# One matmul per distinct piece in the state picks, and the FFN tiles' transposes two blocks later

## What is computed

```python
def cell(h, x):
    gi = x @ W_ih + b_ih
    gh = h @ W_hh + b_hh
    i_r, i_z, i_n = jnp.split(gi, 3, axis=-1)
    h_r, h_z, h_n = jnp.split(gh, 3, axis=-1)
    r = jax.nn.sigmoid(i_r + h_r)
    z = jax.nn.sigmoid(i_z + h_z)
    n = jnp.tanh(i_n + r * h_n)
    h_new = (1.0 - z) * n + z * h
    return (h_new, h_new)
...
qx, sx, sc = _reorder_quantize_x(xf, up_reorder_index)
g = _qlinear(qx, sx, sc, w_gate, up_reorder_index, out_idx=down_reorder_index)
u = _qlinear(qx, sx, sc, w_up, up_reorder_index, out_idx=down_reorder_index)
t = jax.nn.silu(g) * u
qt, st, sct = _reorder_quantize_x(t, down_reorder_index)
y = _qlinear(qt, st, sct, w_down, down_reorder_index)
...
x = x + y
```

## Time and profile before

| what | us |
|---|---|
| median of 3 runs (2846.30 to 2849.53) | 2847.83 |
| the profiled execution | 2844.01 |
| its span, first to last instruction | 2842.2 |
| TensorE matmul busy in it | 2554.6 |
| VectorE busy | 1686.3 |
| GpSimd busy | 1252.9 |
| ScalarE busy | 1139.7 |
| one-add product of t = 2, 3, 4, 5 (from the first pick to the last block) | 98.4, 101.8, 99.5, 105.0 |

### The profile page before, as it was taken

The page is one execution under the profiler, slowest core; times in us unless marked ns, Lnnn a source line. Parts: engine busy times, 40 slices in busy tenths (PEclk is TensorE's granted clock), DMA queues, the critical chain, the costliest instruction groups (busy, mean ns, idle before and its releaser), DMA issues. The chain is left out here.

```text
span 2842.2 us, 154419 instructions
## 1 busy us (share of the span) xinstructions
PE 2554.6 (90%) x67605; PEld 1655.8 (58%) x67605; DVE 1686.3 (59%) x3398; ACT 1139.7 (40%) x2317; POOL 1252.9 (44%) x598
## 2 busy tenths in 40 slices
PE   2088999999989999999999999999896999999996
PEld 1066777777767778777665664755642444444442
DVE  8852222224822222225737879867492888888887
ACT  1312222225722222225602333323233777777774
POOL 0256666663146666665161450713601233333334
PEclk8599999999999999999999999999998999999998
DMA  6833222224622222225664353443432223232322
GB/s 196 241 82 82 71 72 74 71 71 107 146 69 71 72 74 71 71 75 138 191 143 122 109 144 113 125 153 97 146 121 95 71 86 95 79 96 84 95 64 54
DMA packets 234857, 293.97 MB, mean 103 GB/s; under 512 B 69581, under 2 KB 194023, under 8 KB 233895
## 3 DMA queue, kind: packets, MB, share of 16 engines
q1 hardware_dynamic: 212743, 240.84, 31.3%
q10 hardware_dynamic: 18304, 36.19, 3.7%
q0 software_dynamic: 3680, 15.21, 1.9%
HBM read 231.61 MB, written 60.45 MB: 103 GB/s over the span
## 5 line engine op out<-in xcount | busy, mean ns | idle before, releaser
L1161 PE MATMUL psum<-second_shared 64*32 64x384 f16 x32768 | 1029.5, 325 | 48.1 <-issue 28.3
L1169 PE MATMUL psum<-low_w,low_hot 64*32 64x384 f16 x16384 | 819.1, 325 | 5.6 <-issue 5.6
L1407 DVE TENSOR_SCALAR second_shared<-psum 32x384 f16<-32x384 f32 x496 | 272.4, 549 | 754.1 <-PE psum L1161 746.8
L1161 PEld LDWEIGHTS psum<-second_shared 64*32 64x32 f16 x32768 | 594.5, 93 | 209.6 <-issue 78.8
L971 POOL TENSOR_TENSOR low_hot<-first_shared,sum_mask 128x1024 f16<-128x1024 f16 x256 | 504.5, 1971 | 425.0 <-DVE first_shared L1394 165.4
L965 POOL TENSOR_TENSOR second_shared<-first_shared,whole_mask 128x2048 f16<-128x2048 f16 x128 | 462.3, 3612 | 447.3 <-PE psum L1161 352.3
L1061 ACT ACTIVATE second_shared<-psum 32x384 f16<-32x384 f32 x496 | 239.4, 483 | 807.5 <-PE psum L1161 801.5
L1249 PE MATMUL psum<-low_w,low_hot 64*64 64x384 f16 x12288 | 513.9, 325 | 12.6 <-issue 6.5
L1249 PEld LDWEIGHTS psum<-low_w,low_hot 64*64 64x64 f16 x12288 | 373.9, 108 | 146.2 <-issue 10.0
L1169 PEld LDWEIGHTS psum<-low_w,low_hot 64*32 64x32 f16 x16384 | 315.7, 93 | 66.3 <-issue 7.1
L2037 PE MATMUL psum<-first_shared,hT 128*64 128x256 f32 (+1 forms) x1856 | 314.6, 492 | 0.0
(11 more groups left out here) (286 smaller groups left out, 2667.5 us busy)
## 6 DMA issues: line engine op xcount, KB each, us to landing
low_w<-w_rows SPq DMA_DIRECT2D x384, 144.0 KB
low_w<-w_rows SPq DMA_DIRECT2D x256, 120.0 KB
second_shared<-w_rows SPq DMA_DIRECT2D x1024, 24.0 KB, 1.8
x_gates<-x_out ACTq DMA_DIRECT2D x58, 384.0 KB, 2.4
xg<-x_gates SPq DMA_DIRECT2D x58, 384.0 KB, 3.2
low_w<-w_rows SPq DMA_DIRECT2D x256, 72.0 KB
low_w<-w_rows SPq DMA_DIRECT2D x384, 48.0 KB
w_rows<-quantised SPq DMA_DIRECT2D x24, 384.0 KB, 4.9
```

The costliest lines, as they stand in the source:

```text
L1161: last = nc.tensor.matmul(run[m][u][j * Q:(j + 1) * Q, :], whole_hot[rows[u], m, sign, kk, j % 2 * Q:(j % 2 + 1) * Q], whole_w[rows[u], m, ...
L1169: nc.tensor.matmul(run[m][u][j * Q:(j + 1) * Q, :], low_hot[rows[u], m, kk, j % 2 * Q:(j % 2 + 1) * Q], low_w[rows[u], m, at:at + UC], sta ...
L1407: last = nc.vector.tensor_scalar(whole_w[u * B:u * B + Q, m, 0, bq, :], run[m][u][bq * Q:(bq + 1) * Q, :], 1.0 / HIGH_ONE, None, ALU.mult)
```

## The change

Two things. First, in the picks of t = 2 to 5 the kinds that occur several times, A0 (four rows) and A1H (three rows), get a selector of their own, sum_sel, which holds the ones of all their rows; A2H keeps its window into low_sel. A pick is then three matmuls instead of eight, with the same sum. sum_sel lies in the part of quantised (qdn) that holds the rounded w_down from t = 5 on. GpSimd fills it between the two pair products, with a memset and 14 casts, and the first pick waits for it (sel_ok). Second, turn_pair and turn_down are called inside a four, ahead of its third block, instead of ahead of the first.

```diff
+            SUM_KINDS = (A0, A1H)
+            sum_sel = qdn[:, 0:2 * PB * P // D, :].rearrange("p k n -> p (k n)").rearrange("p (a g r) -> p a g r", a=2, g=PB)
...
+                sel_ok = ssem("sel_ok")
...
                         pair_hots(0)
+                        pool.wait_ge(hot_ok, block_no(2, 0, 0) + 1)
+                        nc.gpsimd.memset(sum_sel, 0.0).then_inc(sel_ok, 1)
+                        pool.wait_ge(sel_ok, 1)
+                        eights = ident[:].rearrange("p (n k) -> p n k", k=SK)
+                        for r, kind in enumerate(SUM_ROWS):
+                            if kind in SUM_KINDS:
+                                for sub in range(SUBS):
+                                    at = sub * B + r * SK
+                                    nc.gpsimd.tensor_copy(sum_sel[:, SUM_KINDS.index(kind), :, at:at + SK], eights[:, sub::SUBS, :]).then_inc(sel_ok, 1)
                         pair_hots(1)
...
                         def sum_chain(t, m, behind=None):
-                            def four(n, ahead):
+                            def four(n, ahead, turn_tile=None):
 
                                 for j in range(BUFS):
+                                    if turn_tile and j == BUFS // 2:
+                                        turn_tile()
...
-                                turn_pair(first)
-                                four(2, 0)
+                                four(2, 0, lambda: turn_pair(first))
                                 with pe.Fori(first + 1, tiles[-1] + 1) as tile:
-                                    turn_pair(tile)
-                                    four(tile, 2 - first)
+                                    four(tile, 2 - first, lambda: turn_pair(tile))
                             else:
                                 with pe.Fori(0, KD) as n:
-                                    turn_down(n)
-                                    four(n, 2)
+                                    four(n, 2, lambda: turn_down(n))
                                 turn_columns()
...
                         def pick(t, first=0, last_one=None):
                             pe.wait_ge(cut_h, CUTS * t)
+                            if t == FINE:
+                                pe.wait_ge(sel_ok, 1 + SUBS * sum(kind in SUM_KINDS for kind in SUM_ROWS))
                             for n in range(first, places(t) if last_one is None else last_one):
                                 group, whole = pick_of(t, n)
                                 if whole:
-                                    shift, kinds, pick_rows = WHOLE_SEL, WHOLE_ROWS, whole_sel[:, group]
+                                    rows = [(kind, whole_sel[:, group, WHOLE_SEL - r * SK:WHOLE_SEL - r * SK + P]) for r, kind in enumerate(WHOLE_ROWS)]
+                                elif t < FINE:
+                                    rows = [(kind, low_sel[:, group, LOW_SEL - r * SK:LOW_SEL - r * SK + P]) for r, kind in enumerate(LOW_ROWS)]
                                 else:
-                                    shift, kinds, pick_rows = LOW_SEL, LOW_ROWS if t < FINE else SUM_ROWS, low_sel[:, group]
+                                    rows = [(kind, low_sel[:, group, LOW_SEL - r * SK:LOW_SEL - r * SK + P]) for r, kind in enumerate(SUM_ROWS)
+                                            if kind not in SUM_KINDS]
+                                    rows += [(kind, sum_sel[:, n_kind, group, :]) for n_kind, kind in enumerate(SUM_KINDS)]
...
-                                for row, kind in enumerate(kinds):
-                                    last = nc.tensor.matmul(psum[:, SEL_BANKS[n % SELS], 0:KD * B], pick_rows[:, shift - row * SK:shift - row * SK + P],
+                                for r, (kind, pick_rows) in enumerate(rows):
+                                    last = nc.tensor.matmul(psum[:, SEL_BANKS[n % SELS], 0:KD * B], pick_rows,
                                                             a_split[:, kind].rearrange("p g b -> p (g b)"),
-                                                            start=row == 0, stop=row == len(kinds) - 1)
+                                                            start=r == 0, stop=r == len(rows) - 1)
                                 last.then_inc(selected, 1)
```

## The result

The kernel with the change takes 2824.27 us in the median of five runs (2817.68 to 2830.37), the kernel before 2846.30 beside it. The ratio is 0.9928, 95% interval 0.9905 to 0.9950: 20.5 us faster, with 14 to 27 in the interval (the two medians alone are 22.0 apart). The forecast was 2828.6, 19.2 us faster. The total came out as forecast; three of its terms did not (less waiting for tiles than forecast, more slow clock, less gain at t = 2), and their errors nearly cancel.

What follows compares the result with a forecast made beforehand. TensorE was taken to set the end through the products of t = 2 to 5. Picks 12.2, transposes 7.0 and 0 for the rest make 19.2 us, so 2847.8 - 19.2 = 2828.6 us; range 2819 to 2840.

Steps and rivals of the forecast that it cites:

- Picks, behind blocks 0 and 1: Picks 3 to 7 of t = 2 to 5: 25 matmuls fewer save 2.9 us a product.
- Ahead of block 0: Picks 0 to 2: ScalarE's store holds the start at t = 3 to 5; only t = 2 gains 0.58 us.
- Transposes: Each tile's turn is asked for 5.26 us later: 7.0 us of TensorE's 14.1 us of tile waits go.
- 39.3 us: VectorE's time from the end of tile 1 to tile 4 at t = 3, leaving 1.2 us of waiting.
- At t = 5: Four w_down tiles: VectorE falls back 9.4 us with 4.7 in hand, leaving 4.7 us of waits instead of 7.3.
- Clock: Four start gaps and one tile wait make 2 falls to 1.2 GHz, 3.4 us, as many as now: net 0.
- two in five: Share of TensorE waits of 2.41 to 2.74 us followed by the lower clock; one fall costs 1.7 us.
- The start gap: TensorE's wait ahead of block 0 grows from 1.41 us to 2.5 to 2.8, in four places.
- The third rival: Every start gap ahead of block 0 drops the clock: 6.8 us instead of 2.7, time 2832.7; chance 0.10.
- Selectors: GpSimd's memset and 14 casts take 3 to 30 us, hidden in an idle stretch of 94.05 us: cost 0.
- The second rival: VectorE runs in the slow order, 13.98 us a tile, with 15.2 us of waits: 8.4 us gained, 2839.4; chance 0.15.
- the prediction's sign that t = 0 and 1 don't move: The prediction is wrong if the products of t = 0 and 1 move.

Runs made afterwards that it cites:

- the two kernels with less lead: The change with the transposes ahead of a four's second block, or in the middle of it: ratios to the kernel before 0.9947 and 0.9936.
- the two kernels above: The change with t = 5's w_down transposes two blocks later still, or ahead of blocks 10, 15, 21, 26: ratios to the kernel before 0.9928 and 0.9890.
- the kernel with w_down two blocks later: The change with the four w_down transposes of t = 5 two blocks later still: ratio to the kernel before 0.9928.

## Why the prediction was right, and where not

For t = 3 to 5 the prediction's terms make 8.7 + 7.0 + 0 = 15.7 us, and 15.8 were measured. As measured below, the terms are 8.9 + 9.5 - 3.4 = 15.0, with 0.8 us not placed; that the sums are so near is luck. By its steps:

**Picks, behind blocks 0 and 1.** 2.9 us a product forecast, 2.70 to 2.73 in each of the four. Right: the next hot was there, and no wait stands at block 1 or 3. Ahead of block 0, nothing was forecast at t = 3 to 5 and 0.24 us each was found; ScalarE's store holds the start nearly, not wholly. The wait for it inside the picks is 0.22 us.

**Transposes.** The step that failed is the pace at t = 3 and 4, "39.3 us" for three tiles against 33.2 asked. These 39.3 hold two tiles of 14 us; a VectorE that is held keeps 11.1, 33.2 for the three, and even where it isn't held, in the two kernels with less lead, they take 36.5. So 0 us of wait was left instead of 1.2 twice. At t = 5, 4.7 us were forecast and 4.56 measured, in part by luck: 3.4 us were in hand instead of 4.7, and VectorE fell back by 7.9 us over two tiles instead of 9.4 over three, because behind the wait TensorE was slow and VectorE's next tile took only 13.1 us. That two more blocks of lead leave this wait and a slower asking removes it is shown by the two kernels above. Waits: 9.5 us gone instead of 7.0.

**Clock.** The step that failed is the rate, "two in five". It was taken from waits of 2.41 to 2.74 us for a tile and put on the starts. The start gap became 2.41 us at t = 3 to 5 and 2.63 at t = 2, where 2.5 to 2.8 were forecast, but all four starts of the profiled run fell, 1.5, 1.4, 1.6 and 1.5 us, and the last tile wait as well, 2.0. Against it stand the falls of before that went with their waits: 1.7 at t = 3 and 1.5 at t = 5. At t = 3 to 5 that is a loss of 3.4 us where 0 was forecast. The third rival's falls thus came true for that run, with a chance of 0.10; its time, 2832.7, did not, since fewer tile waits were left. Over the ten traces the gap of 2.41 us at t = 3 to 5 was followed by the lower clock in 12 of 18 cases and the gap of 1.41 us in none of 12; two in five was too few. The page "TensorE: Matmul & The Clock Gate" of the Trainium skill, section "HAM oscillation — how this bites in real kernels", has the half rate come back behind every wait of a kernel that waits some 3 to 5 us at a time for a DMA. The gaps here are shorter, 2.41 us, and the traces agree in 12 of 18 cases.

**The product of t = 2.** 3.5 us forecast, 1.8 measured, and 0.6 ahead of it. The picks there save the same 2.73 us, block 0 starts 0.33 us earlier where 0.58 were forecast, and it lost 1.5 to the clock: here too the clock is the step that failed. Beyond that this product varies with its weights: across the ten traces it takes 96.6 to 105.3 us, with and without the edits. In six of the eight experiments block 0 waits there for the weights, as in the one with the picks alone:

```profile
1416.72 3.66 PE L1263 MATMUL psum<-low_w,low_hot 64*64 64x384 f16 x44 [4.29 <-DMA low_w<-w_rows]
```

In the change's own trace it waits for the hot, 2.63 us, though the DMA engines are fully taken from 1402 to 1409.9 (share 1.04 at 328 GB/s), as they were before (1.03 at 348 GB/s from 1402 to 1410.5). The prediction carried the wait of the earlier trace rows at t = 3 over to t = 2 and left the transfers out.

**Selectors.** Nothing forecast, nothing found: 4.4 us in a wait of 94.

**The second rival**, that the order of VectorE's and GpSimd's instructions decides and a later transpose creates no time, had 0.15. At t = 3 and 4 the order turned out well; at t = 5 it is what the kernel with w_down two blocks later ran into. The Trainium skill, page "SBUF — State Buffer", section "Who interferes with whom", has a VectorE instruction with two SBUF inputs and a GpSimd instruction that reads SBUF exclude each other; the 1.61 and 3.31 us of L1455 with GpSimd still and at work agree.

The rest of the 19.8 us between the two profiled spans, 2842.2 and 2822.4, is 0.6 us ahead of t = 2 and some 1.6 behind t = 5. Of the change only the selectors lie there, and single traces differ by more: from the second pair product's first hot to the first pick of t = 2 it is 639.5 us before, 642.7 with the change and 632.5 to 642.2 in the other eight. So these 2.2 us can't be put down to the change, and the prediction's sign that t = 0 and 1 don't move can't be read this finely.

## What to carry to other kernels

Work taken off the bounding engine is worth its time only if what it waits for next is early as well: in single traces the picks alone gave nothing, and 3.8 us on top of the moved transposes. Where one engine asks for what another makes, compare the two paces before moving the asking: lead cures a short lateness, but when the maker is slower in every round a fixed lead is used up, and here asking at the maker's pace removed the wait. And before shortening the work ahead of a wait on TensorE, look at what the longer gap does to its clock: where the clock fell, 15 matmuls that nobody needed were cheaper than the gap (0.24 us against 1.4 to 1.7); where it kept, they cost those 0.24 us.

## What was not expected of the hardware

- The same gap, 2.41 us ahead of block 0 behind the same three picks, was followed by 1.2 GHz in 12 of 18 cases and by 2.4 GHz in 6. What tells them apart no row here shows. Behind 1.34 to 1.41 us it kept its level in 13 of 13.
- Two engines that disturb each other settled into a fixed pattern where the transpose held VectorE: 11.07 to 11.08 us a tile, TensorE's own pace, for all tiles of t = 3 and 4 behind tile 1 in six kernels, against 8.5 to 14.1 without.
- A cast of 128x64 on GpSimd took 0.18 us (14 in 2.56 us) and a memset of 128x2048 1.80 us.
